# Recurrence of a gated unit on TensorE: each product's moving columns repeated to sixteen by an access of stride zero

## The reference, cut to what matters

```python
def cell(h, x):
    gi = x @ W_ih + b_ih
    gh = h @ W_hh + b_hh
    i_r, i_z, i_n = jnp.split(gi, 3, axis=-1)
    h_r, h_z, h_n = jnp.split(gh, 3, axis=-1)
    r = jax.nn.sigmoid(i_r + h_r)
    z = jax.nn.sigmoid(i_z + h_z)
    n = jnp.tanh(i_n + r * h_n)
    h_new = (1.0 - z) * n + z * h
    return (h_new, h_new)
```

## Time and profile before

| what | value |
|---|---|
| median of 3 runs | 4085.2 us (4082.55 to 4085.6) |
| the profiled execution | 4082.55 us |
| its span, first to last instruction | 4080.8 us |
| mean granted TensorE clock over the span | 0.811 |
| PE busy | 3714.3 us (91%), 70140 products |
| PEld busy | 2790.9 us (68%) |
| DVE busy | 2751.6 us (67%) |
| ACT busy | 2083.0 us (51%) |
| POOL busy | 485.9 us (12%) |
| recurrence | from 1088.5 us, 512 steps |

### The profile page before, as it was taken

How to read it: one execution, slowest core, us unless ns; L and a number is a source line. 1 busy time by engine, 2 the same in 40 slices (tenths; PEclk the granted TensorE clock), 3 DMA queues, 4 the chain that set the end, 5 groups by cost and what they waited for, 6 DMA issues and landing times. The chain is left out here.

```text
span 4080.8 us, 177523 instructions
## 1 busy us (share of the span) xinstructions
PE 3714.3 (91%) x70140; PEld 2790.9 (68%) x70140; DVE 2751.6 (67%) x10621; ACT 2083.0 (51%) x7371; POOL 485.9 (12%) x427
## 2 busy tenths in 40 slices
PE   2458888887999999999999998999999999999999
PEld 2425565553599999999999996565456546644664
DVE  8878788785677777777777776476367537653762
ACT  4028677677755555555555553453245315532542
POOL 2006365365000000000000000001000100010001
PEclk9989999998855555555555556999999999999999
DMA  2022132231000000000000003211221141023102
GB/s 93 1 89 94 48 110 84 62 107 55 3 6 6 6 6 6 6 6 6 6 6 6 6 6 137 79 45 42 109 91 33 42 160 50 23 83 124 44 13 93
DMA packets 113885, 203.27 MB, mean 50 GB/s; under 512 B 44076, under 2 KB 76844, under 8 KB 111416
## 3 DMA queue, kind: packets, MB, share of 16 engines
q1 hardware_dynamic: 113720, 201.00, 14.7%
HBM read 160.05 MB, written 32.52 MB: 47 GB/s over the span
## 5 line engine op out<-in xcount | busy, mean ns | idle before, releaser
L1518 PE MATMUL gru_sum_n<-gru_state_parts,w_hh_hi 128*128 128x8 f16 x8192 | 499.6, 174 | 0.0
L1508 PE MATMUL gru_sum_n<-gru_state_parts,w_hh_lo 128*128 128x4 f16 x8192 | 488.9, 168 | 0.0
L1518 PEld LDWEIGHTS gru_sum_n<-gru_state_parts,w_hh_hi 128*128 128x128 f16 x8192 | 376.5, 104 | 0.0
L1508 PEld LDWEIGHTS gru_sum_n<-gru_state_parts,w_hh_lo 128*128 128x128 f16 x8192 | 376.5, 104 | 0.0
L653 ACT ACTIVATE dit_prob<-dit_bank,dit_head_nbias 128x512 f32<-128x512 f32 x256 | 176.0, 688 | 351.1 <-DVE dit_head_nbias L671 350.7
L1651 DVE TENSOR_TENSOR_SCAN gru_n_in<-gru_reset_gate,gru_sum_n 128x32 f32<-128x32 f32 x1024 | 225.5, 220 | 54.3
L1508 PE MATMUL gru_sum_rb<-gru_state_parts,w_hh_lo 128*128 128x4 f16 x4096 | 261.0, 168 | 0.0
L1518 PE MATMUL gru_sum_za<-gru_state_parts,w_hh_hi 128*128 128x8 f16 x4096 | 254.1, 168 | 0.0
L1518 PE MATMUL gru_sum_ra<-gru_state_parts,w_hh_hi 128*128 128x8 f16 x4096 | 254.1, 168 | 0.0
L1518 PE MATMUL gru_sum_zb<-gru_state_parts,w_hh_hi 128*128 128x8 f16 x4096 | 254.1, 168 | 0.0
L1508 PE MATMUL gru_sum_ra<-gru_state_parts,w_hh_lo 128*128 128x4 f16 x4096 | 252.1, 166 | 0.0
(11 more groups left out here) (328 smaller groups left out, 12366.1 us busy)
## 6 DMA issues: line engine op xcount, KB each, us to landing
dit_w_qk<-w_qk_parts SPq DMA_DIRECT2D x64, 512.0 KB, 3.6
room<-w_parts SPq DMA_DIRECT2D x8, 4096.0 KB, 12.2
room<-w_v_parts SPq DMA_DIRECT2D x5, 4096.0 KB, 12.2
room<-w_out_parts SPq DMA_DIRECT2D x4, 4096.0 KB, 13.9
small_given_w<-in_L_cond_qkv_w SPq DMA_DIRECT2D x48, 256.0 KB, 3.2
w_qk_parts<-small_parts_w SPq DMA_DIRECT2D x32, 256.0 KB, 2.1
small_given_w<-in_L_cond_ffn_w SPq DMA_DIRECT2D x32, 256.0 KB, 3.7
w_parts<-small_parts_w SPq DMA_DIRECT2D x32, 256.0 KB, 2.4
```

What stands on the lines that cost most here:

```text
L1508: mm = pe.matmul(columns[:, j, 0], w_hh[1][:, k, c:c + P], parts[:, par, 0, k, :, LAST], start=opens, stop=False, skip_group_check=True)
L1518: mm = pe.matmul(columns[:, j], w_hh[0][:, k, c:c + P], parts[:, par, :, k, :, LAST], start=opens, stop=False, skip_group_check=True)
```

## The change

The moving side of every `high` and `low` product reads the same columns again and again, through one more dimension of stride zero, until there are sixteen: four times the 4 columns of `low`, twice the 8 of `high`. The output has one more dimension too, with 64 floats from one copy to the next, so that the copies' sums go to other columns of the same bank (64 to 79, 128 to 143, 192 to 207 for the gates). Nobody reads them. Copy 0 lies where the sums lay before, so DVE and ACT read what they read before. `bring` stays as it is.

```diff
--- before.py
+++ after.py
@@ -1433,6 +1433,7 @@
         gi_now = [m.sb(f"gi_now_{v}", [P, NOW, 2, KD, 2, B], F16) for v in range(2)]
 
         LAST, GATED = 2, 3
+        WIDE, SPACING = 16, 64
         state = m.sb("state", [P, 2, KD, B, 3])
         parts = m.sb("state_parts", [P, 2, 2, KD, B, 3], F16)
         reset = m.sb("reset_gate", [P, KD, B, 4])
@@ -1494,18 +1495,22 @@
 
             def gate_columns(bank):
 
-                return bank[:, 0:HALF * 2 * B].rearrange("p (f e b) -> p f e b", e=2, b=B)
+                copies = bank[:].rearrange("p (r x) -> p r x", x=SPACING)[:, :, 0:HALF * 2 * B]
+                return copies.rearrange("p r (f e b) -> p r f e b", e=2, b=B)
 
             def new_columns(par, half):
 
-                return n_terms[:, par, half, :, :, 0:2].rearrange("p f b e -> p f e b")
+                copies = n_banks[:, par, half].rearrange("p (r x) -> p r x", x=SPACING)[:, :, 0:HALF * B * 4]
+                return copies.rearrange("p r (f b s) -> p r f b s", b=B, s=4)[:, :, :, :, 0:2]\
+                             .rearrange("p r f b e -> p r f e b")
 
             def low(columns, gate, fs, ks, par, opens=False):
 
                 for j, f in enumerate(fs):
                     for k in ks:
                         c = (gate * KD + f) * P
-                        mm = pe.matmul(columns[:, j, 0], w_hh[1][:, k, c:c + P], parts[:, par, 0, k, :, LAST],
+                        again = parts[:, par, 0:1, k, :, LAST].broadcast_to([P, WIDE // B, B])
+                        mm = pe.matmul(columns[:, 0:WIDE // B, j, 0], w_hh[1][:, k, c:c + P], again,
                                        start=opens, stop=False, skip_group_check=True)
                         opens = False
                 return mm
@@ -1515,7 +1520,9 @@
                 for j, f in enumerate(fs):
                     for k in ks:
                         c = (gate * KD + f) * P
-                        mm = pe.matmul(columns[:, j], w_hh[0][:, k, c:c + P], parts[:, par, :, k, :, LAST],
+                        again = parts[:, par, :, k, :, LAST].rearrange("p (r e) b -> p r e b", r=1)\
+                                                            .broadcast_to([P, WIDE // (2 * B), 2, B])
+                        mm = pe.matmul(columns[:, 0:WIDE // (2 * B), j], w_hh[0][:, k, c:c + P], again,
                                        start=opens, stop=False, skip_group_check=True)
                         opens = False
                 return mm
```

## The result

The changed kernel takes 4090.86 us (4085.16 to 4093.07, 19 runs), the kernel before 4083.58 us in the same series (4080.4 to 4087.76, 19 runs): a ratio of 1.0016 with a 95% interval of 1.001 to 1.0022. By the ratio that is 6.5 us slower (the two medians differ by 7.3). It lies inside the 0.2% that I called no change and 3 us from the forecast of 4088.3, but the interval lies wholly above 1, so something real costs 4 to 9 us, and my sum has only 3.1 us for it. The experiments are about that difference, and about the clock.

A forecast was written before the change was run, and what follows sets the result against it. It took the step's chain through `ra_sum`, DVE and ACT as the bound, 0.06 us over PE's own total. 4082.55 + 3.1 = 4085.7 us, 4088.3 on the median's footing, all other terms 0; range 4044 to 4104.

The forecast's parts named there:

- Pace at the present clock: Recurrence products: 16 columns still fit into the 26.7 ns between starts, covered by the weight load; 0 us.
- The scattered writes of the `n` products: `n` banks: sixteen columns lying apart cost 24 ns, still under 26.7; 0 taken, up to +166 us.
- the rival that the change does nothing: Copies not streamed one by one: 4082.55 us; chance 0.60 together with the forecast.
- The clock, no rise: Recurrence: TensorE's granted clock stays at 0.50, as rises were seen only behind wide products; 0 us taken.
- The price of 80 ns: Full clock's gain per step: 47 intervals shortened by 1.7 ns each, from 26.7 to 25.0; 38 us after subtracting 6 ns.
- the ring: One step's dependent chain, 2.74 us: 48 products to `ra_sum`, then DVE and ACT by turns, back to PE.
- My rival of full clock throughout: Clock 1.00 in the whole recurrence: 4043.6 us, or 4046 on the median's footing; chance 0.09.
- the 33-column bursts: Attention before the recurrence, 431 to 435 us: said to run alone before the clock fell, evidence against a lasting rise.
- na's is covered by the sigmoid that the same scan waits for: First half's `n` sum: its later end is hidden behind ACT's sigmoid, so it adds nothing.
- last product's way: +3.1 us: Last product of `ra_sum`: its record grows from 168 to 174 ns, 6 ns x 512 steps.
- by 20 ns at most: Ends of `na_sum`, `nb_sum` and the other sums come later by this much; not charged.
- The slower rival: Scattered `n` products outgrow the weight load by 3 ns each: 4101 us, 4104 on the median's footing; chance 0.19.

The follow-up runs named there:

- e3: The changed kernel with the last four low products of `na_sum` back at 4 columns: 4087.26 us, 1.0001 of the kernel before.
- e5: The changed kernel with sixteen unread 512-column products ahead of the recurrence: 4090.16 us, 1.0011 of the kernel before.
- e8: The kernel before with 40 columns in gates' low products, 24 in high, 16 in `n` (na's last low ones 4): 4063.01 us, ratio 0.9939.
- e1: The kernel before with 16 columns in the products of gates r and z only, `n` unchanged: 4086.4 us, ratio 0.9999.
- e9: The kernel before with the low `n` products that signal `na_sum` moved four products earlier: 4075.32 us, ratio 0.997.
- e4: The kernel before with 48 columns in the products of gates r and z, `n` unchanged: 4417.71 us, ratio 1.0811.
- e6: The kernel before with gates' low products at 40 columns, high 24, `n` 16 (na's last low 4), plus sixteen 512-column products ahead: 4061.3 us, ratio 0.9932.
- e7: The kernel before with gates at 40 columns, high ones reordered, `n` 16 (na's last low 4), sixteen 512-column products ahead: 4077.35 us, ratio 0.9971.

## Why the prediction was right, and where it was not

*Pace at the present clock, 0: right.* 16 columns keep the intervals: the 47 to the last of `ra_sum` take 1275 ns in before and 1276 in after.

*The scattered writes of the `n` products: right on the pace, wrong on the rest.* The record was priced at 168 + 18 = 186 ns and has 188. In e3 28 of the 32 stay wide and cost nothing. The Trainium skill (PSUM — Partial Sum Buffer, "Specifications (TRN2)") says that non-contiguous access slows matmuls; the records agree (188 ns against the 174 and 177 of the gates' products, also of 16 columns) and the pace does not. The longer records also answer the rival that the change does nothing: the copies were streamed.

*The clock, no rise: right, with too high a price.* It stayed at 0.50, and e5 shows that full clock would not have held. The price of 80 ns took the 25.0 ns of the small attention's products for those of the recurrence; these have 25.8 to 26.4 at full clock, so 35 ns on the 47 intervals and 41 on the 63 that the ring has. My rival of full clock throughout would have given some 21 us (41 x 512; e8's recurrence is 22.6 us shorter), not 38. The sentence of the Trainium skill ("TensorE: Matmul & The Clock Gate", "Why this matters for your kernels") fails here in one more way: in e5 PE was busy without a pause at the upper clock (2.00 of 2.00 us in each window) and lost it. That run is also the better evidence, for I misread: between 431 and 435 not only the 33-column bursts ran, two groups of wide transposes stand among them, PE was busy for only 0.60 to 0.86 of each us, and at 434.87, just ahead of the fall, another run of transposes began.

```profile
431.14 0.66 PE L635 MATMUL small_bank<-ident,small_prob 128*128 128x128 f32 x4 [0.23 <-ACT small_prob L756]
...
434.87 3.54 PE L975 MATMUL small_bank<-ident,small_attended 128*128 128x128 f32 x16
```

So those rows did not show a fall under unbroken thin work. (In the earlier trace rows PE also dips once behind the eleventh slice: the 25th reads 8.)

*The step that failed: "na's is covered by the sigmoid that the same scan waits for".* It is the other way round: the sigmoid is covered by `na_sum`, by 36 ns (68 less the 32 of an open handover). So the ring was not 48 products and then DVE, but 64 products and then the scan: 1702 ns for 63 intervals, 275 to the scan, 254 to the tanh, 250 to the state's scan and 266 to PE's first low product make 2747, the step. With it fell the sum's only term, "last product's way: +3.1 us": the end of `ra_sum` is hidden (e1: 0.9999), and in its place stands the end of `na_sum`, 20 ns of a scattered write, in three steps of four: 20 x 384 = 7.7 us, measured 6.6. I had worked out that very number ("by 20 ns at most") and put it beside the path. That the time still came out 3 us from the forecast is luck: the two ends, the one that I charged and the one that was paid, differ by only 14 ns. The rows would have shown it: 0.07 us where every other handover has 0.03.

*The slower rival.* Its place (the `n` banks) was right, its mechanism wrong: no product outgrew its weight load. Four `n` products take 0.11 us in after, and the pause ahead of the first low product (from the start of the last `bring`) grew from 84 to 104 ns instead of vanishing.

**Still open:** why the scan starts 107 ns behind the end of na's record, when a sum of `ra` follows its last record by 38 ns. The scan has two waits in a row and the sum has one; that alone doesn't explain it, since e9 has the same two and a gap of 32 ns behind the sigmoid, and the order of the two was not tried. Which of the three widths of e8 the clock needs was not tried either, nor whether the spacing of the copies, 32 floats in e4 and e6 to e8 and 64 in e5, plays a part.

## What to carry to other kernels

Where an instruction waits for two signals, compare its handover with the others of the same pair of engines: a gap twice as long is a sign that the signal you follow is not the last one, and a run that shortens the other alone settles it (e3). Then everything that lengthens the other is on the path. A product whose end nobody waits for, or whose signal is covered by a later one (e1), may grow for nothing; the one whose signal comes last costs its full extra length, so keep exactly that one narrow (e3) or early (e9). Padding products to lift the clock pays only with a width that holds it (e5) and does not yet slow the products (e4), and what it gives is read from the pace of the same products at full clock, not of others.

## What the runs showed of the hardware that was not expected

- PE busy for 499.86 to 500.00 of 500 us had a clock of 0.50 with 4, 8 or 16 columns and of 1.00 with 40, 24 and 16 mixed (e8). Twice the clock shortened 47 intervals of such products from 1275 to 1240 ns, by 2.7%.
- At full clock a 48-column product took 30 ns in the low form and 44 ns in the high one (e4), while 40 columns took 26.8 ns in either form with the other reading order (e7).
- The low `n` products' record grew from 168 to 188 ns with sixteen scattered columns in place of four, 14 ns above the 174 of a gate's low product of sixteen, and the distance to the next product stayed at 26.7 ns.
- An ACT instruction that starts right behind another has a record of 0.20 us instead of 0.22 (the tanh in e9 and in the earlier trace rows), so that a tanh 29 ns later in e9 (scan to tanh 254 to 283) took only 11 of the 36 ns: from the tanh to the state's scan it is 233 ns there, before 250.
